# Indirect passes written out with constant waits, and staging copies dropped, in a four-layer graph network kernel

## The reference

```python
x = _layernorm(x + _L0_gnn_ref(x, rFeatures, relation_weights, loop_weight, deg_isqrt, src, dst, edge_type_40))
x = _layernorm(x + _L1_gnn_ref(x, edge_index, W, att_src, att_dst, bias, fc_w, fc_b))
x = _layernorm(x + _L2_gnn_ref(x, edge_index, W_proj, score_src, score_tgt, W_skip, bias))
x = _layernorm(x + _L3_gnn_ref(x, edge_index))
```

## Time and profile before

| | us |
|---|---|
| median of three runs | 12146.04 |
| profiled execution | 12153.88 |
| its span | 12152.0 |
| product pass, layer-0 pass | 422 to 1680, 1710 to 3120 |
| source_maximum, edge pass of layer 2, first_round | 3300 to 4830, 5912 to 7430, 7565 to 9070 |

### The profile page before, as it was taken

The page is one execution under the profiler, slowest core; times in us unless marked ns, Lnnn a source line. Parts: engine busy times, 40 slices in busy tenths (PEclk is TensorE's granted clock), DMA queues, the critical chain, the costliest instruction groups (busy, mean ns, idle before and its releaser), DMA issues. The chain is left out here.

```text
span 12152.0 us, 198157 instructions
## 1 busy us (share of the span) xinstructions
PE 6929.4 (57%) x41381; PEld 5175.5 (43%) x41382; DVE 7092.0 (58%) x19002; ACT 3369.7 (28%) x10770; POOL 5647.4 (46%) x5161
## 2 busy tenths in 40 slices
PE   4444433333366666787455553555547777777775
PEld 3211112222222222444344442444437676767675
DVE  7422235454554544777544445444448888888888
ACT  0000000000100000121111111333337776777775
POOL 0466656666255554333355553555543343434342
PEclk9767765555655555998655555666669999999998
DMA  0222234444355556554122222333345454545454
GB/s 21 79 105 107 112 95 104 103 105 102 72 156 155 154 155 144 186 180 131 45 58 58 58 58 47 95 97 95 96 86 164 143 163 142 164 143 163 143 163 122
DMA packets 1108605, 1387.92 MB, mean 114 GB/s; under 512 B 277722, under 2 KB 974382, under 8 KB 1108142
## 3 DMA queue, kind: packets, MB, share of 16 engines
q1 hardware_dynamic: 955182, 1090.46, 28.7%
q0 software_dynamic: 153344, 296.65, 11.9%
HBM read 1002.58 MB, written 383.96 MB: 114 GB/s over the span
## 5 line engine op out<-in xcount | busy, mean ns | idle before, releaser
L2097 POOL TENSOR_TENSOR msg_r<-zo_r,ex_r 128x1024 f32<-128x1024 f32 x580 | 1121.6, 1934 | 1878.2 <-ACT ex_r L2184 1878.2
L2192 ACT ACTIVATE hots_r<-zo_r,tot_r 128x128 f32<-128x128 uint8 x4640 | 1416.5, 387 | 576.0 <-DVE tot_r L2137 389.4
L2225 PE MATMUL ps<-msg_r,hots_r 128*128 128x128 f32 x9280 | 1195.2, 282 | 573.9 <-ACT hots_r L2192 461.4
L2225 PEld LDWEIGHTS ps<-msg_r,hots_r 128*128 128x128 f32 x9280 | 1087.6, 193 | 681.5 <-DVE u_sum L2150 666.5
L598 POOL DMA_INDIRECT ring_e<-t_tab,st_e x880 | 831.1, 944 | 893.5 <-DVE st_e L590 597.2
L2213 PE MATMUL ps<-u,wide_r 128*128 x9280 | 1143.2, 277 | 169.2 <-ACT wide_r L2177 164.8
L1879 POOL DMA_INDIRECT z_r<-x_tab,st_r x880 | 833.9, 948 | 808.3 <-issue 441.2
L477 POOL DMA_INDIRECT rec_tab<-st_pay,st_row x832 | 808.6, 972 | 858.3 <-DVE st_pay L529 596.7
L2213 PEld LDWEIGHTS ps<-u,wide_r 128*128 128x128 f32 x9280 | 1093.8, 194 | 171.8 <-issue 171.7
L1078 POOL DMA_INDIRECT ring_m<-t_tab,st_m x880 | 842.8, 958 | 684.9 <-issue 349.4
L598 POOL DMA_INDIRECT ring<-y_tab,st x880 | 883.4, 1004 | 550.5 <-DVE st L590 290.4
(11 more groups left out here) (316 smaller groups left out, 13040.7 us busy)
## 6 DMA issues: line engine op xcount, KB each, us to landing
zo_r<-zo_tab SPq DMA_DIRECT2D x2320, 192.0 KB, 2.6
y_tab<-y_out SPq DMA_DIRECT2D x250, 512.0 KB
k_tab<-ring_m SPq DMA_DIRECT2D x220, 520.0 KB
ring_e<-k_tab SPq DMA_DIRECT2D x220, 520.0 KB
ohts_e<-oht_tab SPq DMA_DIRECT2D x440, 128.0 KB
zo_tab<-z_r SPq DMA_DIRECT2D x220, 256.0 KB
dl_b<-dl_tab SPq DMA_DIRECT2D x220, 128.0 KB
oht_tab<-ohts SPq DMA_DIRECT2D x220, 128.0 KB
```

Source lines behind the costliest of these rows:

```text
L2097: nc.gpsimd.tensor_tensor(msg[:, s % WR].rearrange("p c (k d) -> p c k d", d=CD), z_of(s).rearrange("p c (k d) -> p c k d", d=CD), ex[:, s ...
L2192: last = nc.scalar.activation(hots[:, s % WR, c, :], rows[:, c, :], ACT.Copy, scale=tot[:, s, c:c + 1])
L2225: last = nc.tensor.matmul(ps[:, 4 + s % 2, c // 2 * D:(c // 2 + 1) * D], hots[:, s % WR, c, :], msg[:, s % WR, c, :], start=c % 2 == 0, st ...
```

## The change

`sweep` gets an argument `straight`; with it the loop is unrolled while the kernel is built, so that every wait and every ring index is a constant. It is set in the layer-0 pass, source_maximum, the edge pass of layer 2 and first_round, on all their engines. The product pass and the scatter are written out in the same way. Tile numbers are still read into registers, once per four quads. The staging buffers, their semaphores and their copies go: gathers take their addresses from y_row or src_row in place, and the scatter takes row_i and pay. The scatter loses its bounds check; edges which it had skipped by an address out of range get a row of their own behind the table.

```diff
-def sweep(eng, stages, tiles=None, count=NQ):
+def sweep(eng, stages, tiles=None, count=NQ, straight=False):
...
-    with eng.Fori(first, last) as i:
+
+    def turn(i):
         if tiles is not None:
             tiles.load(i * RING + tiles.offset, RING)
         for s in range(RING):
             for off, fn in stages:
                 fn(i * RING + (s + off), (s + off) % RING)
+    if straight:
+        for i in range(first, last):
+            turn(i)
+    else:
+        with eng.Fori(first, last) as i:
+            turn(i)
...
-                    with pool.Fori(0, HB // 2) as i:
-                        for s in range(2):
-                            pool.wait_ge(s_st, i * 4 + (2 * s + 2))
-                            pool.sem_inc(s_tick, 1)
-                            for j in range(SU):
-                                nc.gpsimd.indirect_dma_start(
-                                    out=rec_tab, out_offset=bass.IndirectOffsetOnAxis(ap=st_row[:, s, j:j + 1], axis=0),
-                                    in_=st_pay[:, s, j, :], in_offset=None,
-                                    bounds_check=SLOTS - 1, oob_is_err=False).then_inc(s_sc[s], 16)
...
+                    for j in range(EJ):
+                        nc.gpsimd.indirect_dma_start(
+                            out=rec_tab, out_offset=bass.IndirectOffsetOnAxis(ap=row_i[:, j:j + 1], axis=0),
+                            in_=pay[:, j, :], in_offset=None).then_inc(s_sc, 16)
...
-                nc.vector.tensor_copy(st[:, s, :], rows[:, bass.ds(q * CQ, CQ)]).then_inc(s_stage, 1)
...
             def gather(q, s):
-                pool.wait_ge(s_stage, q + 1)
-                if not isinstance(q, int) or q >= RING:
+                if q >= RING:
                     pool.wait_ge(s_free, q - (RING - 1))
-                pool.sem_inc(s_tick, 1)
                 for c in range(CQ):
                     nc.gpsimd.indirect_dma_start(
                         out=ring[:, s, c, 0:width], out_offset=None, in_=table,
-                        in_offset=bass.IndirectOffsetOnAxis(ap=st[:, s, c:c + 1], axis=0)).then_inc(s_gath[s], 16)
-            return stage, gather
+                        in_offset=bass.IndirectOffsetOnAxis(ap=rows[:, q * CQ + c:q * CQ + c + 1], axis=0))\
+                      .then_inc(s_gath[s], 16)
+            return gather
...
-                    sweep(dve, [(3, stage), (1, hot), (0, add), (0, turned_hot), (0, hot_bytes)], tiles)
+                    sweep(dve, [(1, hot), (0, add), (0, turned_hot), (0, hot_bytes)], tiles, straight=True)
```

More of the change, by code:

```diff
@@ L805, in keep_bytes @@
                           .then_inc(s_bst[s], 16)
-                    sweep(sp, [(2, targets), (0, keep), (0, keep_bytes)])
+                    sweep(sp, [(2, targets), (0, keep), (0, keep_bytes)], straight=True)
                     for s in range(RING):
@@ L813, in _ @@
                     pool.wait_ge(s_ini, 2)
-                    _, gather = stage_and_gather(None, pool, y_tab, y_row, ring, st, s_stage, s_gath, s_sum, D)
-                    sweep(pool, [(0, gather)])
+                    gather = gather_quads(pool, y_tab, y_row, ring, s_gath, s_sum, D)
+                    sweep(pool, [(0, gather)], straight=True)
                 @block.vector
@@ L868, in total @@
                         last.then_inc(s_sum, 1)
-                    sweep(pe, [(0, total)])
+                    sweep(pe, [(0, total)], straight=True)
         with Phase() as ph:
@@ L1059, in keep @@
                                          ring[:, s, :, 0:W]).then_inc(s_keep[s], 16)
-                        sweep(sp, [(0, keep)])
+                        sweep(sp, [(0, keep)], straight=True)
                         for s in range(RING):
@@ L1123, in top @@
                             return one
-                        sweep(dve, [(3, stage), (0, reduce(0)), (0, reduce(1)), (0, top(0)), (0, reduce(2)),
-                                    (0, top(1)), (0, reduce(3)), (0, top(2)), (2, other), (0, top(3))], tiles)
+                        sweep(dve, [(0, reduce(0)), (0, reduce(1)), (0, top(0)), (0, reduce(2)), (0, top(1)),
+                                    (0, reduce(3)), (0, top(2)), (2, other), (0, top(3))], tiles, straight=True)
                     @block.scalar
@@ L1141, in line @@
                             nc.scalar.activation(lines[:, s, :], turned(s), ACT.Copy).then_inc(s_line, 1)
-                        sweep(act, [(2, pack), (1, line)])
+                        sweep(act, [(2, pack), (1, line)], straight=True)
                     @block.tensor
@@ L1541, in add @@
                             return one
-                        sweep(dve, [(3, stage), (1, sent), (-1, add(0)), (0, score), (-1, add(1)), (-1, add(2)),
-                                    (0, top), (-1, add(3)), (0, message)], tiles)
+                        sweep(dve, [(1, sent), (-1, add(0)), (0, score), (-1, add(1)), (-1, add(2)),
+                                    (0, top), (-1, add(3)), (0, message)], tiles, straight=True)
                         dve.wait_ge(s_acc, NQ * CQ)
@@ L1568, in hot @@
                                                  ACT.Copy).then_inc(s_hot, 1)
[L1569 removed]
+                        sweep(act, [(0, hot), (0, shift)], straight=True)
                     @block.tensor
@@ L1863, in keep @@
                                       .then_inc(s_zst[s], 16)
-                                sweep(sp, [(3, hots_in), (0, keep)])
+                                sweep(sp, [(3, hots_in), (0, keep)], straight=True)
                             body(0)
@@ L1940, in body @@
                                 round_link = linker(dve, s_l, r * LINKS)
-                                sweep(dve, [(4, stage), (-2, add(0)), (1, product), (-2, add(1)), (0, share_inverse),
-                                            (-2, add(2)), (1, reduce), (-2, add(3)), (0, message)], tiles)
+                                sweep(dve, [(-2, add(0)), (1, product), (-2, add(1)), (0, share_inverse), (-2, add(2)),
+                                            (1, reduce), (-2, add(3)), (0, message)], tiles, straight=True)
                                 dve.wait_ge(s_acc, (r + 1) * (CQ * NQ))
```

154 lines of the change are left out of this document (55 added, 99 removed).

## The result

The changed kernel takes 11961.32 us in the median of four runs (11954.99 to 11962.10), the kernel before 12152.43 over the four runs beside them: a ratio of 0.9841, 95% interval 0.9824 to 0.9858. It is faster by 191 us, where 396 were forecast.

The account below looks back on a forecast made before the run. Bound by POOL's runs alternating with stalls; terms -60 - 100 - 160 - 40 - 40 + 1 = -399 against 12153.9 us profiled, giving 11755 us, about 11750 in the median; range 11100 to 12300.

Parts of the forecast that it names:

- What bounds the kernel: All five passes: no engine is full; POOL's uninterrupted runs slow the others, then POOL pauses while they catch up.
- the 1667 us that the change "can touch": POOL's idle time over five passes: scatter 191, layer 0 243, source_maximum 417, layer 2 415, capsules 401 us.
- The product pass, -60: Products and scatter without staging waits: between +93 (late products stay at 5.4 us) and -204 (slowness goes), middle taken.
- Layer 0, -100: Layer-0 gathers: without the copy POOL starts up to 3.8 of 6.6 us sooner, 141 us; -100 taken, between 0 and -243.
- source_maximum, -160: source_maximum gathers: 315 us of idle time end with the copy; half taken, between 0 and -417.
- Layer 2, -40: Layer-2 gathers: only the copy and its register steps go, 0.2 us per quad; between 0 and -120.
- Capsules, -40: Capsule round: the copy's removal gives nothing, shorter steps -40 us; between 0 and -401.
- rival C: Slower: POOL's longer runs take the others' recovery, first in the product pass; 12170 to 12450 us, chance 0.25.
- B: Rival: the slowness hangs on the loops' register steps and goes with them; 10900 to 11500 us, chance 0.21.
- D: Rival: written-out code needs about 350 instruction packets, 145 us if half stall 1 us; chance counted within A's 0.46.
- The rule on copies: DVE copies lock GpSimd out of the shared port; removing them would speed POOL's issues, at most some 150 us in four passes.
- A: As forecast: part of POOL's pauses goes; 11500 to 12120 us, likeliest 11750, chance 0.46 with D's share.

Follow-up runs that it names:

- the six groups: Follow-up kernels, each group on one chip beside the kernel before, which took 12154, 12248, 12227, 11123, 12215 and 12246 us.
- the variant with both pauses: Changed kernel plus POOL waiting after every 12 scatters for 16 products, and before every second capsule-round quad: ratio 1.0071 on the 11123 us chip, 0.9551 on another.

## Why the prediction was wrong

**What bounds the kernel** was read rightly for four of the five passes: waits that POOL doesn't need won 245 us in the scatter and 103 in the capsule round, and without the slowness layer 0 and source_maximum run at nearly POOL's pace, so the alternation of runs and stalls is real. On the one chip where the stalls are absent before takes over 1000 us less, which fits the 1667 us that the change "can touch". Layer 2 is the exception: it takes 1456 us there and 1460 elsewhere, so its 415 us of idle time don't come from the slowness; the prediction's own paragraph on layer 2 puts them to its chain. SyncE's issue is not 0.70 us throughout late in a run, as was read from one row: between 2293 and 2309 us its steps, issues, moves and register steps alike, take 0.01 or 0.7 us each, where register steps and moves take 0.02 to 0.07 behind the run.

**The product pass, -60, measured +190.** This is the step that failed: "Between +93 and -204 I take -60, the middle." The rows had the answer. With a late product at 5.4 us the sum was +93, with the measured 5.6 us and 1.09 behind the scatter it is 1135 + 300 x 1.09 = 1462 against 1249, +213, and the stretch from the first product measured +190, since the scatter now starts 17 us further ahead of the products, and the first gather follows the end of these sums after 36 us instead of 43. Three things were wrong in it. The lower end came from four additions at 442 us, 22 us into a run; PSUM holds four products, so PE had made these while DVE waited for the scatter, and they prove no pace. The middle value took a register step off by count (5.4 to 4.3 us), as if a product's time were the sum of PE's steps; but PE's steps take 0.05 us each, its records of a product run far ahead of its addition, and what costs is each matmul instruction, by a signal that comes late (twice as many: 10.5 to 11.9 us). And the scatter was costed at 1.257 us an issue by POOL's pace alone; beside the products it took 1135 us, 1.37 an issue, 90 us more than the 1045.

**Layer 0, -100, measured -140.** The mechanism was right for the larger part. 3.8 of 6.6 us of a pause were to go, which gave 141 before it was cut to 100; the mean pause fell from 6.2 to 3.0 us. Of the 140 about 90 are the copies and the rest the constants, which the sum had left in the bounds; that the 141 fits so closely is in part luck.

**source_maximum, -160, measured -162.** The size was right, but not its parts: the copies are worth 106, the constants the rest, and it is the packing that POOL waits for now, not the stored slot.

**Layer 2, -40, measured -49.** The size was right, but none of it is the copy's (1458.0 us with the copies kept, 1459.7 without); it is the constants on the chain.

**Capsules, -40, measured +2.** The copy ended nothing, as said. The shorter steps gave nothing either: the runs got longer, nearly all of 12 gathers where half had been of 8, and so did the pauses. That is the part of rival C that came true outside the product pass.

**The rivals.** C described the loss (a late product above 3.6 us) and had its place and sign right; the gather passes gained more than it allowed, so the kernel did not get slower. B, that the slowness hangs on the loops' register steps, fell: written out, 200 products were made beside the scatter. D, the code: 350 packets were forecast from the 59 of one queue; that queue moved 273 and both together 422, and there is no loss to be seen in the passes with most of the new code. With the sentence of the Trainium skill on straight code ("Runtime: NRT & Kernel Launch", Instruction fetch mechanics), the trace agrees. The rule on copies in the Trainium skill ("SBUF — State Buffer", the "DVE blocks DMA" trap) gave at most 150 us for faster issues. The issues of layer 0 take 1.004 us before and after, and those of before that have a copy beside them 0.944, like those with nothing beside them; for these copies the measurement decides against it. What the copies' removal won (140 to 195 us) came from POOL's waits.

**The range and the total.** 11961 lies in the range and in A's own, but the gain is under half of the forecast, through the one term: with +190 in place of -60 the sum is -149. From there to -191 it is two errors that cancel (layer 0 by -40, the capsules by +42) and 29 us in a stretch that the change does not touch; that part is luck. Of the signs of A, the pauses of 3 us in layer 0 came true, the product pass near its old length did not.

## What to carry to other kernels

A product that arrives late need not have been started late: set the starts of the producer's records beside the waits of the consumer before an engine is called slow. Before a wait is taken from a queue that feeds others, read how the others fare late in its uninterrupted runs; a wait can be what restores them, and taking it away can cost more than it gave (here +190 us), while waits put in won 245 and 103 us. If a range has two ends from the same place, find the row that tells them apart before taking the middle. And measure on more than one chip when a stall can't be explained from the program.

## What the runs showed of the hardware

- Late in a run in which POOL issues indirect transfers without a pause, products of 512 float columns reach DVE only every 4.9 or 5.6 us instead of every 1.03. PE's records start their matmul rows 0.43 to 0.85 us apart all the same; PE's signals are what comes late. The slowness began 12 us into a run in the kernel before, and in the change at 438 us, 32 us behind the first scatter and 14 behind the first product, so its onset is not a fixed length of the run.
- It follows the number of matmul instructions (10.5 to 11.9 us for two halves), not plain PE steps (four more, 0.051 us each: 5.60), and not the rows per transfer (64 rows: 196 products as with 128). Pauses of some 4 us on average after 12 issues bring it to 1.2. The profiled execution took 11961.91 us and the other three 11954.99 to 11962.10, so it does not come from the profiling.
- In layer 0 of the kernel before, an issue of POOL takes 0.944 us with nothing on DVE beside it, 0.944 beside an int32 copy (14 of them), and 1.17 beside DVE's one-hot of line 634 into hots (149 of them).
- It was there wherever before took 12146 to 12248 us (the first comparison and five of the six groups; 200 products beside the scatter in each of the three profiles of the change), and absent on the one chip where before took 11123 us (products at 1.03 us beside the scatter). What differs in that chip, no run shows. What the change itself is worth there was not measured; the variant with both pauses takes 0.7% longer there than the kernel before.
- Why the signals of matmuls come late beside POOL's issues stays open. The DMA engines are far from full (busy share 0.15 in that stretch), half the rows change nothing, and the slowness is there in loops as in written-out code (5.4 and 5.6 us), so code fetch is not it; the trace names no resource.
- The stretch between source_maximum and layer 2, whose code did not change, got 29 us shorter. That was not followed up.
